# Experts kernel: four PSUM buffers for the second layer, the last addition of a tile on GpSimd, one Newton step fewer

## Chip, cores and metric

One core of a Trainium2 chip. The metric is the device time of one execution in microseconds; a version is judged by the median of its runs.

## What is computed

Two layers follow each other on x of 4 x 1024 x 256 (float32). The part that matters is the end of the second layer: a state-space block gives s, a mixture of experts gives g, and the output is x + s * g. Cut to that:

```python
residual = x                                    # xn, 4096 rows of 256
gate_weights = softmax(x @ gate_W + gate_b)     # 8 experts
topk_vals, topk_idx = top_k(gate_weights, 2)
boost = x
for i in range(2):                              # rank 0, rank 1
    h = relu(boost @ W1[e] + b1[e])             # e = topk_idx[..., i], 256 -> 512
    outs[i] = h @ W2[e] + b2[e]                 # 512 -> 256
    boost = boost + 0.5 * outs[i]
fused = topk_vals[0] * outs[0] + topk_vals[1] * outs[1]
g = silu(layer_norm(residual + fused, ln_gamma, ln_beta))
x = x + s * g
```

## The kernel before

The kernel first computes layer 0 (about 0 to 930 us of the profile), then the state-space scan (to about 1930 us), then the experts in two ranks. Only the experts are touched by the change.

Each rank sorts the 4096 rows by their expert and pads them to 39 tiles (NTILE) of 128 rows, every tile of one expert. Every engine has its own program, an order written out by hand, and waits for the others on semaphores.

A tile of a rank goes through these stages. GpSimd gathers its rows by an indirect DMA (first rank L1243, second rank L1276, `second_rows`) into one of six row buffers (NR). TensorE turns the tile (L1881, `turned_in`), ScalarE copies it out of PSUM (L1543) and picks the expert's first weights (L1552). TensorE makes the hidden layer (L1900, `hidden`), ScalarE applies bias and relu (L1561), and TensorE makes the second layer (L1913, `rows_out`) into a PSUM buffer pM2, of which there are two; before it overwrites one it waits on m2c until VectorE has read it. TensorE's order within a tile n is hidden(n + 1), turned_in(n + 2), rows_out(n).

In the first rank VectorE then runs `boost` (L1707, L1709, L1710), and SyncE stores the rows. In the second rank it runs `fuse` (L1726 adds the weighted bias, L1729 adds the product from PSUM, L1731 and L1732 make the statistics) into one of nine buffers f (NF); fuse(n) first waits until the output of tile n - 9 has landed. After every third tile it runs `normalise` on that group of three (GROUP): an inverse square root by a seed (L1736 to L1738) and four Newton steps (L1740 to L1742) on 128 x 3 numbers, then two passes over the three tiles (L1745, L1750). ScalarE applies silu (L1567). `finish` multiplies by s (L1756) and adds x (L1758); both come from `mx`, a ring of eight buffers (NX) that GpSimd fills by an indirect gather (L1281, `last_rows`). VectorE runs finish(n - 6) behind fuse(n), three times behind the last fuse, and three times more at the end. GpSimd scatters the finished tile to the output (L1285, `finished`).

GpSimd's queue in the second rank is a loop: in turn n it gathers the rows of tile n (waiting for turned_in and for fuse of tile n - 6), gathers mx for tile n - 4 (waiting for finish of tile n - 12), and scatters tile n - 12 (waiting for its finish). Turns 12 to 38 have all three, turns 39 to 42 the last two, turns 43 to 50 the scatter alone:

```python
for n in range(NTILE + 2 * LAG):                # LAG = 6
    if n < NTILE:
        second_rows(n)
    if 0 <= n - LAG + 2 < NTILE:
        last_rows(n - LAG + 2)
    if n >= 2 * LAG:
        finished(n - 2 * LAG)
```

The wait of L1284 stands, in the program that is built, on the instruction that loads the register for the scatter's bounds check, ahead of the DMA instruction; the wait of `last_rows` stands on its DMA instruction.

Of the kernel before, what the change touches and what calls it, by code (L numbers as in the profile page):

```python
# [9 lines left out]
ALU = mybir.AluOpType  # L10
# [3 lines left out]
B, L, D = 4, 1024, 256  # L14
P = 128
# [919 lines left out]
NTILE = 39  # L935
# [4 lines left out]
NR, NF, LAG, NX = 6, 9, 6, 8  # L940
# [5 lines left out]
def phase_me(nc, g):  # L946

    AT = half_jobs()
    with ExitStack() as ctx:
# [3 lines left out]
        def sem(name):  # L953
            return ctx.enter_context(nc.semaphore(name))
# [6 lines left out]
        def part(of, at, shape, dt=F32):  # L961

            n = int(np.prod(shape))
            v = of[:, at:at + n]
            v = v if dt is F32 else v.bitcast(dt)
            if len(shape) == 2:
                return v.rearrange("p (a b) -> p a b", b=shape[1])
            if len(shape) == 3:
                return v.rearrange("p (a b c) -> p a b c", b=shape[1], c=shape[2])
            return v  # L970
# [48 lines left out]
        e_w2 = [xi[:, :, :].rearrange("p m t -> p (m t)")[:, 0:E * D]] + [zu[:, k, :, :].rearrange("p a t -> p (a t)") for k in (1, 2, 3)]  # L1019
        b2 = zu[:, 4, :, :].rearrange("p a t -> p (a t)")  # L1020
        f = part(rows, 0, [NF, D])
        mx = part(rows, NF * D, [NX, 2 * D])
# [11 lines left out]
        row = lambda n: first[:, n % NR, :] if n % NR < 2 else rest[:, n % NR - 2, :]  # L1034
        xsT = tile([2, KD * P]); ws = tile([2, KD * HE]); hT = tile([2, HE])
        st = sb("st_e", [P, 2, GROUP, 6]); mv = sb("mv_e", [P, 2, GROUP, 2]); rs = sb("rs_e", [P, 4, GROUP]); spare = sb("spare_e", [P, 1])

        Q = [ctx.enter_context(nc.psum_tensor(f"m_Q{i}", [P, 2, CH], F32)) for i in range(4)]
        pT1, _, pM2, pT2 = Q
        dA, du, _, Y = (q[:, :, :].rearrange("p a b -> p (a b)") for q in Q)  # L1040
        X = [Q[2][:, i, :] for i in range(2)]
        R0, R1 = Q[3][:, 0, :], Q[3][:, 1, :]
# [15 lines left out]
        t1 = sem("e_t1"); t1c = sem("e_t1c"); picked = sem("e_picked")  # L1058
        t2 = sem("e_t2"); t2c = sem("e_t2c"); m2 = sem("e_m2"); m2c = sem("e_m2c")
        row_ok = sem("e_row_ok"); r1_out = [sem(f"e_r1_out{i}") for i in range(3)]  # L1060
        ln = sem("e_ln"); fn = sem("e_fn"); sl = sem("e_silu"); fin = sem("e_fin"); og_out = [sem(f"e_og_out{i}") for i in range(NF)]; f_out = sem("e_out")

        def tile_at(b, kind, m):
            return b * NQT + (TILES if b else TILES0).index((kind, m))
# [4 lines left out]
        with nc.Block() as block:  # L1069
# [78 lines left out]
            def _(pool):  # L1148
# [90 lines left out]
                def index(r, n, i):  # L1239
                    return bass.IndirectOffsetOnAxis(ap=ext[:, r, n, i:i + 1], axis=0)  # L1240
# [31 lines left out]
                def second_rows(n):  # L1272
                    if n >= NR:
                        pool.wait_ge(t1, NTILE + n - NR + 1)
                        pool.wait_ge(m2c, NTILE + n - NR + 1)
                    nc.gpsimd.indirect_dma_start(row(n), None, g["r1_s"], index(1, n, 0)).then_inc(r_in[n % NR], 16)  # L1276

                def last_rows(n):
                    if n >= NX:
                        pool.wait_ge(fin, 2 * (n - NX) + 2)  # L1280
                    nc.gpsimd.indirect_dma_start(mx[:, n % NX, :], None, g["mx_s"], index(1, n, 1)).then_inc(mx_in[n % NX], 16)  # L1281

                def finished(n):
                    pool.wait_ge(fin, 2 * n + 2)  # L1284
                    nc.gpsimd.indirect_dma_start(g["out"].rearrange("b n d -> (b n) d"), index(1, n, 2), f[:, n % NF, :], None, bounds_check=B * L - 1, oob_is_err=False).then_inc(og_out[n % NF], 16)  # L1285

                for n in range(NTILE + 2 * LAG):
                    if n < NTILE:
                        second_rows(n)
                    if 0 <= n - LAG + 2 < NTILE:  # L1290
                        last_rows(n - LAG + 2)
                    if n >= 2 * LAG:
                        finished(n - 2 * LAG)

            @block.scalar
            def _(ac):
# [288 lines left out]
            def _(dv):  # L1585
                v_ = nc.vector
# [13 lines left out]
                k = [2]  # L1600
# [97 lines left out]
                def boost(n):  # L1698
                    dv.wait_ge(m2, n + 1)
                    if n >= 3:  # L1700
                        dv.wait_ge(r1_out[n % 3], 16 * (n // 3))
                    w = ext[:, 0, n, 3:4].bitcast(F32)
                    if n == 0:
                        dv.wait_ge(b2_in, 16)
                    e = dv.value_load(texp[0:1, 0, n:n + 1], min_val=0, max_val=E - 1)
                    m = out1[:, n % 3, D:]
                    v_.tensor_tensor(m, pM2[:, n % 2, 0:D], b2[:, bass.ds(e * D, D)], ALU.add).then_inc(m2c, 1)  # L1707
                    dv.wait_ge(m2c, n + 1)
                    v_.scalar_tensor_tensor(out1[:, n % 3, 0:D], m, 0.5, row(n)[:, 0:D], ALU.mult, ALU.add).then_inc(row_ok, 1)  # L1709
                    v_.scalar_tensor_tensor(m, m, w, row(n)[:, 0:D], ALU.mult, ALU.add).then_inc(row_ok, 1)  # L1710
# [9 lines left out]
                def fuse(n):  # L1720
                    if n >= NF:
                        dv.wait_ge(og_out[n % NF], 16 * (n // NF))
                    w = ext[:, 1, n, 3:4].bitcast(F32)
                    e = dv.value_load(texp[0:1, 1, n:n + 1], min_val=0, max_val=E - 1)  # L1724
                    dv.wait_ge(r_in[n % NR], 16 * (turns_of[n % NR] + n // NR + 1))
                    link(v_.scalar_tensor_tensor(row(n)[:, D:], b2[:, bass.ds(e * D, D)], w, row(n)[:, D:], ALU.mult, ALU.add))  # L1726
                    dv.wait_ge(m2, NTILE + n + 1)
                    dst = f[:, n % NF, :]
                    v_.scalar_tensor_tensor(dst, pM2[:, (NTILE + n) % 2, 0:D], w, row(n)[:, D:], ALU.mult, ALU.add).then_inc(m2c, 1)  # L1729
                    dv.wait_ge(m2c, NTILE + n + 1)  # L1730
                    link(v_.bn_stats(st[:, n // 3 % 2, n % 3, :], dst))  # L1731
                    link(v_.bn_aggr(mv[:, n // 3 % 2, n % 3, :], st[:, n // 3 % 2, n % 3, :]))  # L1732

                def normalise(q):
                    var, y, y2 = (rs[:, i, :] for i in range(3))
                    link(v_.tensor_scalar(var, mv[:, q % 2, :, 1], EPS, None, ALU.add))  # L1736
                    link(v_.tensor_scalar(y2.bitcast(I32), var.bitcast(I32), 1, None, ALU.logical_shift_right))
                    link(v_.tensor_scalar(y.bitcast(I32), y2.bitcast(I32), -1.0, RSQRT_SEED, ALU.mult, ALU.add))  # L1738
                    for _ in range(4):
                        link(v_.tensor_tensor(y2, y, y, ALU.mult))  # L1740
                        link(v_.scalar_tensor_tensor(y2, y2, -0.5, var, ALU.mult, ALU.mult))  # L1741
                        link(v_.scalar_tensor_tensor(y, y2, 1.5, y, ALU.add, ALU.mult))  # L1742
                    for i in range(GROUP):
                        dst = f[:, (q * GROUP + i) % NF, :]
                        v_.scalar_tensor_tensor(dst, dst, mv[:, q % 2, i, 0:1], gamma[:, 0, :], ALU.subtract, ALU.mult).then_inc(ln, 1)  # L1745
                    c[0] += GROUP
                    dv.wait_ge(ln, c[0])
                    for i in range(GROUP):
                        dst = f[:, (q * GROUP + i) % NF, :]
                        v_.scalar_tensor_tensor(dst, dst, y[:, i:i + 1], gamma[:, 1, :], ALU.mult, ALU.add).then_inc(fn, 1)  # L1750

                def finish(n):
                    dv.wait_ge(sl, n + 1)
                    dv.wait_ge(mx_in[n % NX], 16 * (n // NX) + 16)
                    dst = f[:, n % NF, :]
                    v_.tensor_tensor(dst, dst, mx[:, n % NX, 0:D], ALU.mult).then_inc(fin, 1)  # L1756
                    dv.wait_ge(fin, 2 * n + 1)
                    v_.tensor_tensor(dst, dst, mx[:, n % NX, D:], ALU.add).then_inc(fin, 1)  # L1758

                for n in range(NTILE):  # L1760
                    boost(n)
# [11 lines left out]
            def _(pe):  # L1773
                mm = nc.tensor.matmul
# [87 lines left out]
                for b in range(B):  # L1862
                    for i in range(STEPS):
                        n = b * STEPS + i
                        m, s = divmod(i, NS)
# [38 lines left out]
                def rows_out(r, n):  # L1904
                    q = r * NTILE + n
                    e = pe.value_load(texp[0:1, r, n:n + 1], min_val=0, max_val=E - 1)
                    if q == 0:
                        pe.wait_ge(w2_in, 16 * HE // P)
                    pe.wait_ge(t2c, q + 1)
                    if q >= 2:  # L1910
                        pe.wait_ge(m2c, q - 1)
                    for k in range(HE // P):
                        ins = mm(pM2[:, q % 2, 0:D], hT[:, q % 2, k * P:(k + 1) * P], e_w2[k][:, bass.ds(e * D, D)],  # L1913
                                 start=(k == 0), stop=(k == HE // P - 1))
                    ins.then_inc(m2, 1)

# [77 lines left out]
```

## Time and profile before

| | us |
|---|---|
| median of 3 runs | 2315.36 (2309.3 to 2317.42) |
| the profiled execution | 2311.29 |
| its span, first to last instruction | 2309.6 |
| busy in the span: TensorE | 1934.5 |
| VectorE | 1716.8 |
| ScalarE | 1258.1 |
| GpSimd | 1225.2 |
| mean granted TensorE clock | 0.949 |

The median is what a change is compared with; durations of single instructions come from the profiled execution. Busy shares over the whole span say little about one stage, so the stages of the two ranks are looked at by themselves. PE is TensorE's matmuls, PEld its weight loads, DVE is VectorE, ACT ScalarE, POOL GpSimd, SP SyncE; a number in brackets is the time the engine sat idle before the instruction, and what ended it.

### The profile page before, as it was taken

The page shows a single profiled execution, that of the slowest core. Times are in us where ns is not written, and L with a number is a line of the kernel's source. Part 1 is how long each engine was busy: PE and PEld are TensorE (multiplying, and loading weights), DVE is VectorE, ACT ScalarE, POOL GpSimd, SP SyncE. Part 2 cuts the span into 40 slices and gives each one's busy share as a digit, 9 for nine tenths or more (in the row PEclk, how much of TensorE's full clock was granted, in tenths as well). Part 3 has the DMA queues.
Part 4 walks back from the last instruction along what each step waited for, and adds up shares of the span by engine and source line. Part 5 has one row for each costly group of instructions (what it writes and reads, how often), then busy time and mean ns, then how long its engine had stood idle before and what let it go on. Part 6 is the DMA issues. An engine that isn't in the chain of part 4 may idle for free. (4 is left out here: it accounts for less than half of the span.)

```text
span 2309.6 us, 25591 instructions
## 1 busy us (share of the span) xinstructions
PE 1934.5 (84%) x7956; PEld 1054.0 (46%) x7956; DVE 1716.8 (74%) x2363; ACT 1258.1 (54%) x1646; POOL 1225.2 (53%) x651
## 2 busy tenths in 40 slices
PE   5699879977997899889988998899876678998984
PEld 3335534643464345333324333433332235887873
DVE  4984498369826952699999999999989995333887
ACT  3873486258526741566654666466644334664663
POOL 2601351054106210278879899989986774223664
PEclk9899989999998999999998999999999999999997
DMA  6510641073007311688888988998899993223442
GB/s 163 138 37 0 156 108 29 0 198 76 19 19 182 74 37 47 69 313 282 287 287 295 308 289 262 317 318 283 266 289 377 331 327 132 98 97 106 138 136 79
DMA packets 182695, 402.63 MB, mean 174 GB/s; under 512 B 49454, under 2 KB 78384, under 8 KB 181410
## 3 DMA queue, kind: packets, MB, share of 16 engines
q1 hardware_dynamic: 170530, 371.10, 52.2%
q0 software_dynamic: 12032, 29.90, 4.5%
q8 instruction: 66, 1.08, 0.2%
q14 instruction: 67, 0.55, 0.1%
HBM read 356.30 MB, written 45.51 MB: 174 GB/s over the span
## 5 line engine op out<-in xcount | busy, mean ns | idle before, releaser
L1191 POOL TENSOR_TENSOR late<-late,rows 128x1024 f32<-128x1024 f32 x256 | 603.2, 2365 | 146.7 <-DVE late L1668 135.3
L1841 PE MATMUL m_Q<-late,ident_m 128*128 128x512 f32 x1024 | 526.6, 646 | 153.1 <-POOL late L1191 113.8
L1668 DVE TENSOR_TENSOR_SCAN late<-m_Q,late 128x1024 f32<-128x1024 f32 x256 | 586.3, 2290 | 45.1 <-ACT m_Q L1377 16.6
L1377 ACT ACTIVATE m_Q<-late,acol 128x1024 f32<-128x1024 f32 x256 | 286.1, 1118 | 362.8 <-DVE late L1668 360.6
L1841 PEld LDWEIGHTS m_Q<-late,ident_m 128*128 128x128 f32 x1024 | 194.3, 202 | 452.5 <-POOL late L1191 260.5
L1661 DVE TENSOR_TENSOR late<-m_Q,rows 128x1024 f32<-128x1024 f32 x256 | 307.2, 1200 | 12.8 <-DMA rows<-bc_s 12.6
L290 POOL TENSOR_TENSOR qkh<-early,qkh 128x1024 bf16<-128x1024 f32 x16 | 33.9, 2130 | 287.4 <-ACT qkh L561 287.4
L456 DVE SCALAR_TENSOR_TENSOR early<-early,work 128x1024 f32<-128x1024 f32 x128 | 155.9, 1218 | 25.2 <-ACT early L598 22.7
L1900 PE MATMUL m_Q<-late 128*128 128x128 f32 x1248 | 159.0, 282 | 8.0 <-DVE m_so L1696 0.8
L1900 PEld LDWEIGHTS m_Q<-late 128*128 128x128 f32 x1248 | 148.5, 194 | 32.7 <-issue 31.0
L606 ACT ACTIVATE early<-early 128x1024 f32<-128x1024 f32 x128 | 134.8, 1053 | 47.4 <-DVE early L461 46.1
L607 ACT ACTIVATE early<-early,halfpi 128x1024 f32<-128x1024 f32 x128 | 145.2, 1134 | 0.0
L493 DVE TENSOR_TENSOR s<-work,s 128x1024 f32<-128x1024 f32 x8 | 9.8, 1224 | 172.9 <-PE work L678 172.9
L461 DVE TENSOR_SCALAR early<-early 128x1024 int32<-128x1024 int32 x128 | 125.3, 979 | 4.4
L678 PE MATMUL work<-w,qkh 128*128 128x256 f32 x512 | 112.6, 381 | 10.8 <-ACT qkh L623 10.8
L332 POOL TENSOR_TENSOR rows<-kr 128x1024 f32<-128x1024 f32 x8 | 16.8, 2119 | 194.6 <-DVE kr L449 194.6
L1913 PE MATMUL m_Q<-m_zu,late 128*128 x468 | 115.0, 382 | 0.0
L840 PE MATMUL work<-x2T,w 128*128 128x512 f32 x256 | 111.6, 594 | 1.0 <-ACT x2T L538 1.0
L678 PEld LDWEIGHTS work<-w,qkh 128*128 128x128 f32 x512 | 96.6, 190 | 30.3 <-ACT qkh L623 17.5
L623 ACT ACTIVATE qkh<-work,b1c 128x512 f32<-128x512 f32 x64 | 40.5, 684 | 123.2 <-PE work L840 123.2
L1788 PE MATMUL m_Q<-early 128*128 128x512 f32 x224 | 106.4, 598 | 0.0
L1707 DVE TENSOR_TENSOR late<-m_Q,m_zu 128x256 f32<-128x256 f32 x39 | 16.6, 425 | 111.5 <-PE m_Q L1913 97.4
(231 smaller groups left out, 3375.1 us busy)
## 6 DMA issues: line engine op xcount, KB each, us to landing
rows<-bc_s SPq DMA_DIRECT2D x512, 512.0 KB, 5.7
rows<-st_s SPq DMA_DIRECT2D x64, 384.0 KB, 5.7
st_s<-qkh SPq DMA_DIRECT2D x128, 96.0 KB, 2.4
r_s<-late SPq DMA_DIRECT2D x39, 256.0 KB, 2.0
rows<-st_s SPq DMA_DIRECT2D x32, 256.0 KB, 6.5
xin<-in_x SPq DMA_DIRECT2D x4, 1024.0 KB, 10.2
xres<-in_x SPq DMA_DIRECT2D x4, 1024.0 KB, 7.2
mx_s<-s SPq DMA_DIRECT2D x4, 1024.0 KB, 4.5
```

Source lines behind the costliest of these rows:

```text
L456: v_.scalar_tensor_tensor(fs[:, s % NF_, :], fs[:, s % NF_, :], ROUND, slot(b, *job)[:, :], ALU.subtract, ALU.subtract).then_inc(rr_ok, 1)
L461: v_.tensor_scalar(fc[:, s % NF_, :].bitcast(I32), fs[:, s % NF_, :].bitcast(I32), 0x7FFFFFFF, None, ALU.bitwise_and).then_inc(ra_ok, 1)
L606: A(fs[:, s % NF_, :], fs[:, s % NF_, :], ACT.Sin, scale=-TURN).then_inc(feat_ok, 1)
L607: A(fc[:, s % NF_, :], fc[:, s % NF_, :], ACT.Sin, scale=-TURN, bias=halfpi[:, :]).then_inc(feat_ok, 1)
L678: i = mm(slot(b, *job)[:, t * D:(t + 1) * D], x(k, t), w[:, k, :], start=(k == 0), stop=(k == nk - 1))
L1191: nc.gpsimd.tensor_tensor(pr[:, n % NH, :], h[:, n % NH, :], cb[:, n % NCB, :], ALU.mult).then_inc(pr_ok, 1)
L1377: A(dA[:, :], dt[:, (b * KI + m) % 2, :], ACT.Exp, scale=acol[:, m, i % NS:i % NS + 1]).then_inc(dA_ok, 1)
L1661: v_.tensor_tensor(dB[:, n % 2, :], du[:, :], bb[:, n % NBB, :], ALU.mult).then_inc(dB_ok, 1)
L1668: v_.tensor_tensor_scan(h[:, n % NH, :], dA[:, :], dB[:, n % 2, :], 0.0, ALU.mult, ALU.add).then_inc(h_ok, 1)
L1841: ins = mm(half(Y, c), ident[:, :], half(pr[:, n % NH, :], c), start=False, stop=(n % NS == NS - 1), skip_group_check=True)
L1900: ins = mm(pT2[:, q % 2, m * P:(m + 1) * P], ws[:, q % 2, k * HE + m * P:k * HE + (m + 1) * P], xsT[:, q % 2, k * P:(k + 1) * P], start=(k ...
L1913: ins = mm(pM2[:, q % 2, 0:D], hT[:, q % 2, k * P:(k + 1) * P], e_w2[k][:, bass.ds(e * D, D)], start=(k == 0), stop=(k == HE // P - 1))
```

## The change

It has four parts. The product of the second layer goes to one of four PSUM buffers instead of two, in both ranks, and rows_out(q) waits for the reading of q - 4 instead of q - 2. The second one uses banks that before held a value of the scan. The addition of x in `finish` (L1758) goes from VectorE to GpSimd's `finished`, which now waits for the multiplication, adds, waits for its own addition on a new semaphore (last), and scatters; fin counts one per tile. In GpSimd's turn `finished` goes ahead of `last_rows`, which waits on last. The Newton loop has three steps instead of four.

```diff
-        pT1, _, pM2, pT2 = Q
+        pT1, pM2a, pM2b, pT2 = Q
+        product = lambda q: (pM2a, pM2b)[q // 2 % 2][:, q % 2, 0:D]
...
                 def last_rows(n):
                     if n >= NX:
-                        pool.wait_ge(fin, 2 * (n - NX) + 2)
+                        pool.wait_ge(last, n - NX + 1)
                     nc.gpsimd.indirect_dma_start(mx[:, n % NX, :], None, g["mx_s"], index(1, n, 1)).then_inc(mx_in[n % NX], 16)
 
                 def finished(n):
-                    pool.wait_ge(fin, 2 * n + 2)
+                    pool.wait_ge(fin, n + 1)
+                    nc.gpsimd.tensor_tensor(f[:, n % NF, :], f[:, n % NF, :], mx[:, n % NX, D:], ALU.add).then_inc(last, 1)
+                    pool.wait_ge(last, n + 1)
                     nc.gpsimd.indirect_dma_start(g["out"]...).then_inc(og_out[n % NF], 16)
 
                 for n in range(NTILE + 2 * LAG):
                     if n < NTILE:
                         second_rows(n)
+                    if n >= 2 * LAG:
+                        finished(n - 2 * LAG)
                     if 0 <= n - LAG + 2 < NTILE:
                         last_rows(n - LAG + 2)
-                    if n >= 2 * LAG:
-                        finished(n - 2 * LAG)
...
-                    v_.tensor_tensor(m, pM2[:, n % 2, 0:D], b2[:, bass.ds(e * D, D)], ALU.add).then_inc(m2c, 1)
+                    v_.tensor_tensor(m, product(n), b2[:, bass.ds(e * D, D)], ALU.add).then_inc(m2c, 1)
...
-                    v_.scalar_tensor_tensor(dst, pM2[:, (NTILE + n) % 2, 0:D], w, row(n)[:, D:], ALU.mult, ALU.add).then_inc(m2c, 1)
+                    v_.scalar_tensor_tensor(dst, product(NTILE + n), w, row(n)[:, D:], ALU.mult, ALU.add).then_inc(m2c, 1)
...
-                    for _ in range(4):
+                    for _ in range(3):
...
                     v_.tensor_tensor(dst, dst, mx[:, n % NX, 0:D], ALU.mult).then_inc(fin, 1)
-                    dv.wait_ge(fin, 2 * n + 1)
-                    v_.tensor_tensor(dst, dst, mx[:, n % NX, D:], ALU.add).then_inc(fin, 1)
...
-                    if q >= 2:
-                        pe.wait_ge(m2c, q - 1)
+                    if q >= 4:
+                        pe.wait_ge(m2c, q - 3)
                     for k in range(HE // P):
-                        ins = mm(pM2[:, q % 2, 0:D], hT[:, q % 2, k * P:(k + 1) * P], e_w2[k][:, bass.ds(e * D, D)],
+                        ins = mm(product(q), hT[:, q % 2, k * P:(k + 1) * P], e_w2[k][:, bass.ds(e * D, D)],
```

## Rows read from the trace of the kernel before

**Rows 1.** Busy time (instructions) of each engine in a stretch; PEclk, DMA share, GB/s.

```profile
1943.00:2085.61 142.61, 138.71 (x911) 120.26 (x910) 43.61 (x105) 86.00 (x208) 31.26 (x33) 1.00 0.28 96
2170.34:2268.46 98.12, 83.54 (x546) 73.17 (x546) 85.51 (x273) 58.73 (x148) 63.51 (x63) 1.00 0.46 139
```

**Rows 2.** Chain of waits, first rank: start us, us, what.

```profile
1946.83 2.02 PE m_Q L1900 x16
...
2081.54 2.02 PE m_Q L1900 x16
```

**Rows 3.** Timeline, VectorE in one group of the second rank: start, duration.

```profile
2199.47 0.43 DVE L1756 TENSOR_TENSOR rows<-rows 128x256 f32<-128x256 f32 x1
...
2199.93 0.42 DVE L1758 TENSOR_TENSOR rows<-rows 128x256 f32<-128x256 f32 x1
...
2206.80 0.17 DVE L1740 TENSOR_TENSOR rs_e<-rs_e 128x3 f32<-128x3 f32 x1
...
2207.40 0.16 DVE L1740 TENSOR_TENSOR rs_e<-rs_e 128x3 f32<-128x3 f32 x1
```

**Rows 4.** Timeline, GpSimd: its turn 12 begins, and one unhindered turn.

```profile
2143.35 0.95 POOL L1276 DMA_INDIRECT late<-r_s,ext  x1 [5.12 <-DVE rows L1729]
...
2161.75 0.98 POOL L1276 DMA_INDIRECT late<-r_s,ext  x1 [0.30 <-PE m_Q L1881]
2163.03 0.95 POOL L1281 DMA_INDIRECT rows<-mx_s,ext  x1 [0.30 <-DVE rows L1729]
2164.29 1.02 POOL L1285 DMA_INDIRECT out<-rows,ext  x1 [0.30 <-issue]
```

**Rows 5.** DMA issues from 2170 to 2268 us: count, median us from issue to landing.

```profile
late<-r_s,ext POOLq DMA_INDIRECT x21, 3.7
...
out<-rows,ext POOLq DMA_INDIRECT x21, 2.9
```

**Rows 6.** Groups by line and shape, GpSimd: count, busy us, mean ns of one.

```profile
L293 POOL TENSOR_TENSOR v<-v,bias 128x1024 f32<-128x1024 f32 x8 | 18.8, 2350 | 1.5 <-ACT v L567 1.5
L293 POOL TENSOR_TENSOR xn_a<-xn_a,bias 128x2048 f32<-128x2048 f32 x4 | 18.8, 4690 | 0.3
...
L317 POOL TENSOR_TENSOR rows<-rows 128x1024 f32<-128x1024 f32 x8 | 21.0, 2647 | 0.0
```

**Rows 7.** Timeline, GpSimd: distances between neighbours, in the scan and before it.

```profile
930.25 0.73 POOL L1162 IOTA ent<- 128x32 int32 x5
931.04 0.23 POOL L1164 MEMSET late<- 128x8 f32 x1
...
1603.09 1.00 POOL L1236 DMA_INDIRECT ext_s<-ent,pos  x1 [0.17 <-issue]
1604.12 4.68 POOL L1191 TENSOR_TENSOR late<-late,rows 128x1024 f32<-128x1024 f32 x2
1608.97 1.00 POOL L1236 DMA_INDIRECT ext_s<-ent,pos  x1 [0.17 <-issue]
```

**Rows 8.** Timeline, the last stretch: VectorE's results and the DMAs they release.

```profile
2276.02 0.43 DVE L1758 TENSOR_TENSOR rows<-rows 128x256 f32<-128x256 f32 x1
...
2276.71 0.98 POOL L1281 DMA_INDIRECT rows<-mx_s,ext  x1 [0.65 <-DVE rows L1758]
...
2298.78 0.43 DVE L1758 TENSOR_TENSOR rows<-rows 128x256 f32<-128x256 f32 x1
...
2300.00 1.19 POOL L1285 DMA_INDIRECT out<-rows,ext  x1 [4.43 <-DVE rows L1758]
...
2302.78 0.99 POOL L1285 DMA_INDIRECT out<-rows,ext  x1 [0.30 <-issue]
```

**Rows 9.** VectorE's L461: one beside GpSimd's L317 (timeline), and its group's mean.

```profile
741.50 1.60 DVE L461 TENSOR_SCALAR early<-early 128x1024 int32<-128x1024 int32 x1
...
L461 DVE TENSOR_SCALAR early<-early 128x1024 int32<-128x1024 int32 x128 | 125.3, 979 | 4.4
```

More of the change, by code:

```diff
@@ L1060, in phase_me @@
         row_ok = sem("e_row_ok"); r1_out = [sem(f"e_r1_out{i}") for i in range(3)]
-        ln = sem("e_ln"); fn = sem("e_fn"); sl = sem("e_silu"); fin = sem("e_fin"); og_out = [sem(f"e_og_out{i}") for i in range(NF)]; f_out = sem("e_out")
+        ln = sem("e_ln"); fn = sem("e_fn"); sl = sem("e_silu"); fin = sem("e_fin"); last = sem("e_last"); og_out = [sem(f"e_og_out{i}") for i in range(NF)]; f_out = sem("e_out")
         def tile_at(b, kind, m):
```

## The prediction

> **What bounds the kernel now.** I read the stage windows first, then the chain of waits, then the timelines of single engines. The change touches only the two expert ranks, about the last 370 us. In the first rank TensorE is busy for 138.71 of 142.61 us while VectorE works 43.61; in the second VectorE is busy 85.51 of 98.12 us and TensorE only 83.54 [rows 1]. The chain of waits says the same of the first rank: it is TensorE's, and a tile takes (2081.54 - 1946.83) / 33 = 4.08 us [rows 2]. The second window of rows 1 spans the fusions of tiles 12 to 33, 21 tiles or seven groups of three: 14.02 us per group, 4.67 per tile. The gaps between dependent instructions fill the rest of VectorE's time, so it never really rests. TensorE needs 3 x 4.08 = 12.24 per group and waits for the rest, some 1.8, on the PSUM buffer that fuse has to read first (m2c).
>
> GpSimd is the third engine to look at, since the change gives it work. Its turn is a gather, a gather of last rows and a scatter, 0.98 + 0.95 + 1.02 us with 0.30 ahead of each: 3.85 us when nothing holds it [rows 4]. In a group it needs 11.6 of the 14.02 us.
>
> **Part 1, VectorE's work taken away.** L1758 starts 0.46 us behind L1756 [rows 3]; without it all that follows moves up by that: 1.38 per group. One Newton step is the distance between two starts of L1740, 0.60 us [rows 3]. VectorE then needs 14.02 - 1.98 = 12.04 us per group, 4.01 per tile, just under TensorE's 4.08.
>
> **Part 2, four PSUM buffers.** The wait of rows_out moves from two to four tiles back, so the stall of 1.8 goes. With VectorE under TensorE's pace, two buffers would nearly do as well: I put nothing extra on it. In the first rank the wait never binds, for VectorE rests there; cost and gain 0. If only parts 1 and 2 counted, the 35 tiles behind the first group would take 4.08 instead of 4.67, and the end would come some 20 us earlier.
>
> **Part 3, GpSimd's addition.** Its turn becomes gather, addition, wait on its own semaphore (last), scatter, gather of last rows. Four prices:
> - The addition, 128x256. The same line costs 2350 ns for 1024 elements and 4690 for 2048 [rows 6], in proportion with nothing fixed, so 256 would be 0.59 to 0.60 us. Beside a busy VectorE the additions of L317 took 2647 for 1024 [rows 6], 1.13 times. As L1726, L1745, L1750 and L1756 will lie beside it, I take 0.66; lower end 0.59.
> - The start behind a gather: 0.03 (1603.09 + 1.00 to 1604.12) [rows 7].
> - From the addition to the scatter. Nothing in this trace waits on GpSimd itself before an indirect DMA, so it is bounded. A DMA that has nothing to wait for starts 0.17 behind an addition (1604.12 + 4.68 to 1608.97) [rows 7]. The gather of last rows, which waits directly, starts 0.27 after VectorE's result (2276.02 + 0.43 to 2276.71), but the scatter L1285, where the wait stands ahead of an instruction that loads its bounds, started at 2300.00 after a result at 2298.78 + 0.43 = 2299.21: 0.79 [rows 8]. The new wait stands in that very place, so the price is near 0.79. A tenth of it is VectorE's signal (0.27 against 0.17 without a wait), while a GpSimd instruction that waits for GpSimd starts some 0.06 behind it (930.25 + 0.73 to 931.04) [rows 7]; I take that tenth off, about 0.70. Ends: 0.17 and 0.82. Nothing can hide this gap: the queue is in order.
> - What it replaces: the 0.30 ahead of the scatter.
>
> A turn is then 0.98 + 0.03 + 0.66 + 0.70 + 1.02 + 0.30 + 0.95 + 0.30 = 4.94 us, over TensorE's 4.08 and over today's 4.65. GpSimd becomes the bound, and the moved order (finished ahead of last_rows) changes nothing in this sum: the gather of last rows waits for the same tile as before, and is needed only two tiles later.
>
> The Trainium skill (SBUF - State Buffer, section "Who interferes with whom") says that a VectorE instruction with two SBUF inputs and a GpSimd instruction that reads SBUF exclude each other, whoever is first. By that rule each of the four VectorE instructions named above could hold the addition off until it ends, and the addition could hold them off for 0.6; it speaks against this change. Of those four the trace shows none beside an addition; its nearest is L461, which took 1.60 us beside GpSimd's L317 against a mean of 0.979 over the kernel [rows 9].
>
> **The sum.** GpSimd is not bound before its turn 12, the first with a scatter; that turn began at 2143.35, when fuse(6) had run [rows 4]. Two norms lie ahead of fuse(6); the first gives back at most 0.4, since fuse(5) waits for its product anyway, the second 0.6: turn 12 starts at 2142.35. From there the queue holds 27 gathers at 1.28, 31 gathers of last rows at 1.25 and 39 scatters at 1.32, less the last 0.30: 124.5 us. Today they are spread until 2302.78 + 0.99 = 2303.77 [rows 8], because VectorE is the bound. The change adds to each of 39 scatters 0.03 + 0.66 + 0.70 - 0.30 = 1.09, 42.5 in all: 2142.35 + 124.5 + 42.5 = 2309.35, **5.6 us later** than 2303.77. What follows the last scatter is the same.
>
> Does anything else hold the queue? The gather of tile n waits for fuse(n - 6). fuse(n) waits for the scatter of n - 9, issued 2.37 us into turn n + 3 and landed 2.9 later [rows 5]; with some 1.8 for value load, L1726 and L1729 it is done about 7.1 into that turn, and turn n + 6 begins at 14.8. The 5 us of a norm fit between. The other way round, a gather needs 3.7 to land [rows 5], and its tile is fused some two turns of TensorE and one product later, about 18 us, 23 with a norm, against six turns of 29.6. At the end turn 38 begins at 2142.35 + 26 x 4.94 = 2270.8, so fuse(38) comes at about 2283 to 2288, and VectorE's last product some 8 us later, before GpSimd's turn for it at about 2302. So GpSimd runs without a pause, and TensorE and VectorE rest in every tile.
>
> The profiled execution took 2311.29 us around a span of 2309.6; the median of the runs is 2315.36, 4.1 above it. I add the difference to the median: 2315.36 + 5.6 = **2321.0 us**. A measurement of this kernel can tell about 0.3% (7 us) from no change, so this is the same time, on the slow side.
>
> **Rivals.**
> - **The addition meets VectorE's instructions (slower).** Place: the addition in each of 39 turns. If half of them wait out an instruction of 0.48, it costs 0.59 + 0.24 = 0.83 or a little more, 0.84: 39 x 0.18 = 7.0 on top, 2328.0. It decides from a mean of 0.695, where the sum passes 7 us. For it: L461 [rows 9]; against: 1.13 is all that L317 shows. [...]
> - **The own wait is cheap (faster).** If the scatter starts 0.30 behind the addition, like every DMA behind another, the turn is 4.54, under 4.65, and 39 x 0.40 = 15.6 us go: 10.0 under the kernel before, 2305.4. With 0.17 it is 2300.3. Against it: 0.79 at the same line.
> - **GpSimd keeps up and TensorE is the bound.** Then some 20 us are gained, 2295. It needs a turn of 4.08, but the three DMAs with the bare addition already are 3.86 + 0.60 = 4.46 less the 0.30 replaced, plus at least 0.20, which is 4.36. Hardly possible.
> - **TensorE loses its clock.** Resting 0.86 us of each 4.94 it could fall to the lower level; at full clock a tile is 4.08, at half about 8. The window of the second rank shows a granted clock of 1.00 with rests of 15% of its time [rows 1]; the rests here are 17%. A few tens of us if it came.
>
> **Chances.** Forecast 0.40; port contention 0.30; cheap wait 0.23; TensorE-bound 0.03; clock 0.04. The forecast's own bounds (addition 0.59 to 0.69, gap 0.66 to 0.76) are 2316.7 to 2324.5, nearly all within 0.3%. Range: 2303.5 to 2329 takes in the cheap wait and the contention. Faster by over 0.3%: 0.26. Within: 0.37. Slower: 0.37.
>
> **What would show it.** After: GpSimd's turn near 4.94 with no wait for another engine from turn 12 on, the scatter 0.70 behind the addition, the addition at 0.66; TensorE waiting for gathered rows rather than for L1729; no time of VectorE's in waits for GpSimd but for landed scatters; the chain of the second rank on GpSimd. Wrong if the gap is 0.3, if additions pass 0.70, or if the chain is still VectorE's.

## The result, and the profile after

The change makes the kernel slower: the median after is 2336.3 us against 2313.3 of the kernel before, run beside it, a ratio of 1.0096 [1.008, 1.0112], 23.0 us. The forecast was 5.6 us slower with an upper end of 2329. The direction was right; the size was four times the forecast and outside the range.

The profiled execution after took 2330.37 us around a span of 2328.2. Line numbers have moved: the scatter is L1288 (was L1285), GpSimd's addition L1286, its gathers L1277 and L1282, the multiplication of `finish` L1759 (L1756), `fuse` L1729 and L1732 (L1726, L1729), the passes of the norm L1748 and L1753 (L1745, L1750), the second layer L1914.

First the busy times over the whole span (busy us, share, instructions), from the page of the kernel after:

```profile
PE 1944.7 (84%) x7940; PEld 1061.8 (46%) x7956; DVE 1710.3 (73%) x2285; ACT 1258.3 (54%) x1646; POOL 1258.2 (54%) x690
```

GpSimd gained 33 us of work and VectorE lost only 6.5, although it was relieved of 39 additions of 0.426 and of a Newton step. The stage windows say more (columns as in [rows 1]):

```profile
1943.00:2082.50 139.50, 135.64 (x888) 117.29 (x886) 42.32 (x102) 85.05 (x206) 31.20 (x33) 1.00 0.29 98
2170.34:2278.00 107.66, 88.51 (x515) 75.00 (x513) 77.72 (x223) 55.05 (x139) 78.50 (x79) 0.94 0.40 119
```

In the first rank TensorE is busy for 97% of the window, as before [rows 1], so the buffers changed nothing that shows there. In the second, VectorE went from 85.51 busy in 98.12 us (87%) to 77.72 in 107.66 (72%); TensorE is busy for 82%. Neither is the bound. GpSimd's busy share is 73% only, and yet it is the bound, as its timeline shows (start, duration, what; in brackets the idle time before it and what ended it):

```profile
2174.90 0.95 POOL L1277 DMA_INDIRECT late<-r_s,ext  x1 [0.30 <-issue]
2175.87 0.73 POOL L1286 TENSOR_TENSOR rows<-rows 128x256 f32<-128x256 f32 x1
2177.44 1.01 POOL L1288 DMA_INDIRECT out<-rows,ext  x1 [0.83 <-POOL rows L1286]
2178.76 0.96 POOL L1282 DMA_INDIRECT rows<-mx_s,ext  x1 [0.30 <-issue]
2180.02 0.95 POOL L1277 DMA_INDIRECT late<-r_s,ext  x1 [0.30 <-issue]
2181.00 0.97 POOL L1286 TENSOR_TENSOR rows<-rows 128x256 f32<-128x256 f32 x1
2182.80 1.01 POOL L1288 DMA_INDIRECT out<-rows,ext  x1 [0.83 <-POOL rows L1286]
```

One turn, from gather to gather, is 5.12 us here (forecast 4.94); the next one, where the addition takes 0.97, is 5.37. All idle time in it is its own: 0.30 between two DMAs, 0.83 between the addition and the scatter. From turn 12 to the last scatter GpSimd waited for another engine for under 1 us of 184. The ends of that stretch:

```profile
2138.41 0.94 POOL L1277 DMA_INDIRECT late<-r_s,ext  x1 [4.53 <-DVE rows L1732]
...
2321.33 0.99 POOL L1288 DMA_INDIRECT out<-rows,ext  x1 [0.80 <-POOL rows L1286]
```

That is 2322.32 - 2138.41 = 183.9 us, against 2303.77 - 2143.35 = 160.4 before [rows 4, 8]: 23.5 more. Turn 12 began 4.94 us earlier than before, but 3.06 of that lies ahead of everything the change touches (the first gather of the second rank started at 2097.45 instead of 2100.51 in this execution); the rest, 1.9, is put down to the change. By that the change costs 23.5 - 1.9 = 21.6 us in these two executions, and 23.0 between the medians.

GpSimd's groups, from the lines of the two ranks (instructions, busy us, mean ns of one, idle us before them and what ended it):

```profile
L1288 POOL DMA_INDIRECT out<-rows,ext x39 | 42.0, 1076 | 32.3 <-POOL rows L1286 32.3
...
L1286 POOL TENSOR_TENSOR rows<-rows 128x256 f32<-128x256 f32 x39 | 34.0, 872 | 1.2 <-DVE rows L1759 0.4
```

The forecast gave the addition 0.66, the gap 0.70, the scatter 1.02. They are 0.872, 32.3 / 39 = 0.83, and 1.076. And VectorE's (in [rows 3] L1759 was L1756 with 0.43):

```profile
L1729 DVE SCALAR_TENSOR_TENSOR late<-m_zu,ext,late 128x256 f32<-128x256 f32 x39 | 22.5, 578 | 40.8 <-DMA out<-rows,ext 29.0 <-DMA late<-r_s,ext 6.3 <-DVE mv_e L1735 3.2
L1748 DVE SCALAR_TENSOR_TENSOR rows<-rows,mv_e,gamma 128x256 f32<-128x256 f32 x39 | 21.0, 592 | 0.5
L1753 DVE SCALAR_TENSOR_TENSOR rows<-rows,rs_e,gamma 128x256 f32<-128x256 f32 x39 | 20.0, 566 | 0.5
L1732 DVE SCALAR_TENSOR_TENSOR rows<-m_Q,ext,late 128x256 f32<-128x256 f32 x39 | 18.9, 484 | 13.9 <-PE m_Q L1914 12.7
L1759 DVE TENSOR_TENSOR rows<-rows 128x256 f32<-128x256 f32 x39 | 18.0, 473 | 1.4 <-ACT rows L1570 0.3
```

The first three were 483, 481 and 481 ns in the kernel before, L1759 was 427, L1732 was 484. So four of the large lines have grown by 46 to 111 ns, 13 us together, and one has not. That one reads PSUM and a single tensor in SBUF; the four read two in SBUF. The growth lies where an addition of GpSimd's lies beside the instruction: L1729 takes 0.54 to 1.27 us in the 15 tiles where one does, and 0.47 to 0.49 in the other 24; L1732 takes 0.48 either way. One such meeting, VectorE's two instructions and the addition:

```profile
2202.70 0.72 DVE L1729 SCALAR_TENSOR_TENSOR late<-m_zu,ext,late 128x256 f32<-128x256 f32 x1 [3.11 <-DMA out<-rows,ext]
2203.03 0.97 POOL L1286 TENSOR_TENSOR rows<-rows 128x256 f32<-128x256 f32 x1
2203.46 0.48 DVE L1732 SCALAR_TENSOR_TENSOR rows<-m_Q,ext,late 128x256 f32<-128x256 f32 x1
```

The waits from 2110 to 2320 (waiting line, what it waited for: us, times, longest):

```profile
POOL out L1288 <- POOL rows L1286: 31.5, 38, 0.9
DVE late L1729 <- DMA out<-rows,ext: 29.0, 14, 3.1
PE m_Q L1882 <- DMA late<-r_s,ext: 13.1, 15, 1.6
```

`fuse` waits for the scatter of tile n - 9 to land, and TensorE waits for gathered rows: both waits are on transfers that GpSimd issues late. The chain of waits of the second rank shows how this looks from the end (start, us, what; its longest pieces):

```profile
2230.89 0.98 POOL rows L1286
2232.70 2.57 DMA out<-rows,ext
2240.50 1.83 DVE rows L1748 x3
...
2247.40 0.99 POOL rows L1286
2249.21 2.57 DMA out<-rows,ext
2257.24 1.76 DVE rows L1748 x3
```

It goes from a scatter's landing to VectorE's norm and back to GpSimd, once in 16.5 us, three of GpSimd's turns. Read alone, it would suggest that VectorE shares the blame. But it comes back from VectorE to GpSimd at the gather L1282, which has 0.30 us of idle time ahead of it there, the same as a DMA that waits for nothing; from turn 12 on VectorE held GpSimd's queue up by 0.4 us in all, and itself rested 29.0 us for landings.

### The profile page after: what moved, and what is told of

It reads as the page before. It is cut to its first block and busy times, and to the rows that moved or that the text cites. A ratio compares the mean times of both kernels' runs of the same rounds, so it can differ in the third digit from the quotient of the medians.

```text
span 2328.2 us, 25534 instructions
## 1 busy us (share of the span) xinstructions
PE 1944.7 (84%) x7940; PEld 1061.8 (46%) x7956; DVE 1710.3 (73%) x2285; ACT 1258.3 (54%) x1646; POOL 1258.2 (54%) x690
## 5 line engine op out<-in xcount | busy, mean ns | idle before, releaser
L1671 DVE TENSOR_TENSOR_SCAN late<-m_Q,late 128x1024 f32<-128x1024 f32 x256 | 586.2, 2290 | 45.1 <-ACT m_Q L1380 16.5
L461 DVE TENSOR_SCALAR early<-early 128x1024 int32<-128x1024 int32 x128 | 124.2, 970 | 4.4
L678 PE MATMUL work<-w,qkh 128*128 128x256 f32 x512 | 112.6, 381 | 10.9 <-ACT qkh L623 10.9
L1914 PE MATMUL m_Q<-m_zu,late 128*128 x468 | 120.3, 396 | 0.0
L1914 PEld LDWEIGHTS m_Q<-m_zu,late 128*128 128x128 f32 x468 | 93.0, 199 | 13.8
```

The source lines that it names most:

```text
L461: v_.tensor_scalar(fc[:, s % NF_, :].bitcast(I32), fs[:, s % NF_, :].bitcast(I32), 0x7FFFFFFF, None, ALU.bitwise_and).then_inc(ra_ok, 1)
L678: i = mm(slot(b, *job)[:, t * D:(t + 1) * D], x(k, t), w[:, k, :], start=(k == 0), stop=(k == nk - 1))
L1671: v_.tensor_tensor_scan(h[:, n % NH, :], dA[:, :], dB[:, n % 2, :], 0.0, ALU.mult, ALU.add).then_inc(h_ok, 1)
L1914: ins = mm(product(q), hT[:, q % 2, k * P:(k + 1) * P], e_w2[k][:, bass.ds(e * D, D)], start=(k == 0), stop=(k == HE // P - 1))
```

## The experiments

Each ratio is to the kernel before on the same chip, with its 95% interval in brackets. On the chip of a to d, e2, m2, n2 and t that kernel took 2311 to 2312 us; p and the first runs of e, m and n were on another.

**a. The addition back on VectorE** (and the old order; four buffers and three Newton steps stay). It separates GpSimd's part from the rest.

```diff
-                    nc.gpsimd.tensor_tensor(f[:, n % NF, :], f[:, n % NF, :], mx[:, n % NX, D:], ALU.add).then_inc(last, 1)
-                    pool.wait_ge(last, n + 1)
...
+                    dv.wait_ge(fin, 2 * n + 1)
+                    v_.tensor_tensor(dst, dst, mx[:, n % NX, D:], ALU.add).then_inc(fin, 1)
```

> Four buffers and three Newton steps kept, the addition back on VectorE and GpSimd's order as before. Theory Q (GpSimd's own in-order turn of 5.3 us is what made the changed kernel slow): the turn falls back to 3.85 and VectorE is the bound with 14.02 - 0.60 = 13.4 us per group; 12 groups x 0.6 = 7 us under the kernel before, about 2306. Rival P (the four buffers or their banks cost something by themselves): 2313 or more.

Measured: 2300.9, 0.9955 [0.994, 0.9969], 10.9 us under the median of the kernel before, and 5 under what was expected. The addition on GpSimd thus costs some 35 us against leaving it where it was, and parts 1 and 2 are a gain. Most groups of three took 13.3 to 13.4 us, against 14.02 less one Newton step of 0.60, 13.42.

**b. No addition at all** (the output lacks x).

```diff
-                    nc.gpsimd.tensor_tensor(f[:, n % NF, :], f[:, n % NF, :], mx[:, n % NX, D:], ALU.add).then_inc(last, 1)
-                    pool.wait_ge(last, n + 1)
```

> The changed kernel with the last addition left out altogether (the output lacks x), so that neither VectorE nor GpSimd pays for it. Theory Q: no engine but TensorE is near its limit, 4.08 us per tile, about 20 us under the kernel before, 2293. Rival L (it is the landing of the scatters, for which fuse waited 29 us in the changed kernel, and the ring of nine buffers that bound it, whatever the addition): VectorE goes on waiting for landings and the time stays near 2313 or above.

Measured: 2287.6, 0.9894 [0.9878, 0.9911], 24 us faster. That is what the change would have been worth had GpSimd's part been free; the forecast had put it at about 20, and the expectation at 2293. Waits for landings (the rival) are not what bound the changed kernel.

**c. The bounds register loaded once.** In the built program the wait on `last` stands on the instruction that loads the register for the bounds check, and the load then stands between the wait and the DMA. Here the register is loaded ahead of the loop, and the wait stands on the DMA itself:

```diff
+                top = pool.to_reg(B * L - 1)
...
-                    nc.gpsimd.indirect_dma_start(... bounds_check=B * L - 1, oob_is_err=False)
+                    nc.gpsimd.indirect_dma_start(... bounds_check=top, oob_is_err=False)
```

> The changed kernel with the bound of the scatter's bounds check loaded into its register once, so that the wait on the own addition stands on the DMA instruction itself. Theory Q: the 0.83 us between addition and scatter fall to 0.2 to 0.3, the addition stays at 0.87; 39 x 0.55 = 21 us less than the changed kernel, about 2315. Rival S (it is the semaphore from GpSimd to itself that takes 0.8): no change, 2336.

Measured: 2316.2, 1.0016 [1.0003, 1.0029], 20 us less than the same kernel with the load in place (d, below). GpSimd's timeline, the addition's line now L1288, the scatter's L1290:

```profile
2174.77 0.99 POOL L1288 TENSOR_TENSOR rows<-rows 128x256 f32<-128x256 f32 x1
2176.03 1.01 POOL L1290 DMA_INDIRECT out<-rows,ext  x1 [0.28 <-POOL rows L1288]
```

The gap fell from 0.83 to 0.28. 39 x 0.55 = 21.5 us were to go, and 19.6 went: nearly each microsecond taken out of GpSimd's queue shows in the time, as it must if that queue is the bound. The edit changes two things at once, where the wait stands and whether a load follows it, and they were not tried apart.

**d. Two buffers again**, all else as changed.

```diff
-        product = lambda q: (pM2a, pM2b)[q // 2 % 2][:, q % 2, 0:D]
+        product = lambda q: pM2b[:, q % 2, 0:D]
...
-                    if q >= 4:
-                        pe.wait_ge(m2c, q - 3)
+                    if q >= 2:
+                        pe.wait_ge(m2c, q - 1)
```

> The changed kernel with two PSUM buffers again. Theory Q: TensorE rests in every tile anyway, so the time is that of the changed kernel, 2336, within 4. Rival P (the buffers decide something): TensorE's old stall of 1.8 us per group comes on top of GpSimd's turns, up to 12 x 1.8 = 21 us, 2357; or, if the banks cost, less than 2332.

Measured: 2335.8, 1.0107 [1.0088, 1.0125], the changed kernel's time as expected. The four buffers do nothing that can be told, good or bad, while GpSimd is the bound.

**e, m, n, p on another chip.** There the kernel before took 2346.6 (no trace of it was kept), and e, m and n show pauses of 3 to 9 us in which TensorE and ScalarE rested, which make their second ranks some 20 to 40 us longer than those of e2, m2 and n2. In p there is one such wait, of 3.6 us. From the waits of n:

```profile
ACT late L1544 <- remote: 50.2, 10, 8.9
```

The trace names no cause for them. A gain or loss of VectorE's can vanish in such pauses, so e, m and n were run again on the first chip, as e2, m2 and n2, with the kernels unchanged. Their first runs are told by their ratios only: e 0.9948 [0.9928, 0.9967], m 0.9979 [0.9965, 0.9992], n 0.9995 [0.9979, 1.0011]. Those of e and n do not agree with e2 and n2: on that chip e was faster than the kernel before, and n was not. What follows on these two holds for the first chip.

> The changed kernel's work, in another order in GpSimd's turn: the addition of tile n - 12 first, then the gather of rows, the gather of last rows, and the scatter last, so that two DMAs lie over the wait (in the last turns the next tile's addition lies over it). Theory Q: the gap of 0.83 is covered, the gather starts about 0.2 behind the addition, so the turn is about 4.65; 39 x 0.7 = 27 us less than the changed kernel, 2309. If the gap is not covered (rival S, GpSimd's sequencer doesn't run ahead of its own wait): 2336.

> As the one before, but only every second addition of the first 30 tiles on GpSimd, 15 of 39, the others on VectorE. Theory Q: VectorE needs 13.35 - 1.5 x 0.46 = 12.7 us per group and GpSimd 3 x 3.85 + 1.5 x 0.8 = 12.8, both near TensorE's 12.2: 4.25 per tile, under the 4.45 of the run with all additions on VectorE; about 6 us less than that one, 2295. Rival C (the exclusion at the port costs VectorE what it is spared: each addition holds it up by up to 0.5): no gain on 2301.

> The kernel before with three Newton steps instead of four, and nothing else. Theory Q: VectorE's group falls from 14.0 to 13.4 us, 7 us in all, the same as with four buffers, 2301 to 2306. Rival P (four buffers bring something of their own while VectorE is the bound): at least 3 us slower than the run a_add_on_vectore.

**p. A write in place of the addition.** `memset` writes zeros to the tile where GpSimd added (the output is zeros). It keeps the turn's shape, with its own wait, but reads nothing from SBUF.

```diff
-                    nc.gpsimd.tensor_tensor(f[:, n % NF, :], f[:, n % NF, :], mx[:, n % NX, D:], ALU.add).then_inc(last, 1)
+                    nc.gpsimd.memset(f[:, n % NF, :], 0.0).then_inc(last, 1)
```

> The changed kernel with the addition replaced by an instruction of GpSimd that reads nothing: it fills the tile with zeros (the output is not the sum). The wait and the scatter stay. Theory C (a GpSimd instruction that reads SBUF and a VectorE instruction with two SBUF inputs exclude each other; it made 0.73 into 0.87 and VectorE's L1729, L1748, L1753 longer): the fill takes its bare 0.46 in every tile and VectorE's three lines are back at 0.48. The turn is 5.34 - 0.41 = 4.93, 16 us less than the changed kernel, 2320. Rival (GpSimd's instructions get longer whatever they do, by the DMAs' traffic): both stay long.

Measured on the second chip: 2313.7, 0.9865 [0.9845, 0.9885]. The durations decide here, not the time. The groups from 2130 to 2330:

```profile
L1729 DVE SCALAR_TENSOR_TENSOR late<-m_zu,ext,late 128x256 f32<-128x256 f32 x33 | 15.9, 483 | 16.7 <-DMA out<-rows,ext 8.5 <-issue 8.1
L1748 DVE SCALAR_TENSOR_TENSOR rows<-rows,mv_e,gamma 128x256 f32<-128x256 f32 x36 | 15.5, 485 | 0.4
L1753 DVE SCALAR_TENSOR_TENSOR rows<-rows,rs_e,gamma 128x256 f32<-128x256 f32 x36 | 15.4, 481 | 0.4
```

They are back at the kernel before's lengths, 481 to 485 (595, 602 and 573 in the changed kernel over the same window). The write took 0.332, and the gap stayed:

```profile
2177.61 1.02 POOL L1288 DMA_INDIRECT out<-rows,ext  x1 [0.83 <-POOL rows L1286]
```

The fill does meet them: 11 of the L1729 lie beside one, and each takes 0.48. So these lines grow by GpSimd's reading of SBUF, and the gap is the same behind an instruction that reads nothing and takes 0.33. The fill itself is shorter than the 0.46 expected.

**e2. The own wait covered.** The addition goes to the front of the turn, so that two gathers lie between it and the scatter (order: addition n - 12, gather n, last rows, scatter n - 12).

```diff
+                def plus(n):
                     pool.wait_ge(fin, n + 1)
                     nc.gpsimd.tensor_tensor(...).then_inc(last, 1)
+
+                def finished(n):
                     pool.wait_ge(last, n + 1)
...
+                    k = n - 2 * LAG
+                    if 0 <= k <= NTILE - NX:
+                        plus(k)
                     if n < NTILE:
                         second_rows(n)
```

> The kernel of e_wait_covered again, on the chance of another chip: in the last four runs, the kernel before among them, the second rank was some 30 us longer than in the runs ahead of them, with up to ten pauses of 3 to 9 us in which ScalarE did nothing though its input was there, so that what they say of GpSimd's turn and VectorE's group is overlaid. Without such pauses, theory Q: GpSimd's turn is 4.5 to 4.6 (addition 0.77, gather 0.16 behind it), VectorE's group 12.1 plus the port's share, so about 4.6 per tile at most: 2300 to 2309, a ratio of 0.995 to 0.999.

Measured: 2312.5, 1.0007 [0.9998, 1.0017], 23 us less than d, but a few us over the upper end of what was expected. From its timeline:

```profile
2196.35 0.76 POOL L1286 TENSOR_TENSOR rows<-rows 128x256 f32<-128x256 f32 x1
2197.27 0.99 POOL L1277 DMA_INDIRECT late<-r_s,ext  x1 [0.16 <-POOL rows L1286]
...
2200.83 0.90 POOL L1286 TENSOR_TENSOR rows<-rows 128x256 f32<-128x256 f32 x1
```

The gap is gone, and a turn is 4.48 here. VectorE's group now sets the pace at least as much as GpSimd's turn, for its instructions meet the additions (its groups; L1755 is the norm's first pass, L1736 the bias line):

```profile
L1736 DVE SCALAR_TENSOR_TENSOR late<-m_zu,ext,late 128x256 f32<-128x256 f32 x39 | 24.6, 632 | 17.6 <-issue 6.7 <-DMA late<-r_s,ext 6.2 <-DVE mv_e L1742 3.2
L1755 DVE SCALAR_TENSOR_TENSOR rows<-rows,mv_e,gamma 128x256 f32<-128x256 f32 x39 | 23.9, 666 | 0.5
```

They are 149 and 185 ns longer than before. VectorE's group is 13.6 us (between the starts of two norms' first passes), three of GpSimd's turns are 13.4: what was lifted off VectorE, 0.43 a tile, it pays back in longer instructions. From 2095 to 2330 us it is busy for 157.45 us, and in n2 (below), which has all 39 additions on it, for 153.61. The expectation had not charged that in full. This is read from the durations; how the missing microseconds divide between the two engines was not tried.

**m2 and t. A part of the additions on GpSimd**, covered as in e2: every second tile of the first 30 (m2, 15 additions), every third (t, 10); VectorE does the others.

```diff
+BY_POOL = range(0, 30, 2)                       # t: range(1, 30, 3)
...
+                def plus(n):
+                    if n in BY_POOL:
+                        pool.wait_ge(fin, n + 1)
+                        nc.gpsimd.tensor_tensor(...).then_inc(last, 1)
```

> The kernel of m_half_of_additions again. Theory Q, without the pauses: VectorE 12.7 us per group plus some 0.2 for the port, GpSimd 12.8: 4.3 per tile, 2293 to 2298, ratio 0.992 to 0.994, below all additions on VectorE (0.9955). Rival C (the port costs VectorE what it is spared): 0.9955 or more.

> As m2_half_of_additions, with one addition in each group of three on GpSimd (10 of 39). Theory Q: VectorE 13.35 - 0.46 + 0.1 = 13.0 us per group, GpSimd 12.4: 4.33 per tile, 2295 to 2300; between half and none.

Measured: m2 2304.8, 0.9979 [0.9968, 0.999]; t 2302.6, 0.9964 [0.9951, 0.9978]. Both expectations were missed (2293 to 2298 and 2295 to 2300), and the rival of m2, that the port costs VectorE what it is spared, came. In the middle of the rank m2's groups of three take 12.7 to 13.0 and 14.2 to 15.2 us by turns, where a's take 13.3 to 13.5. The medians rise with the additions on GpSimd (39: 2312.5, 15: 2304.8, 10: 2302.6, none: 2300.9); 10 is not to be told from none.

**n2. The Newton step alone**: the kernel before with one line changed.

```diff
-                    for _ in range(4):
+                    for _ in range(3):
```

> The kernel of n_newton_alone again. Theory Q, without the pauses: 0.6 us less in 12 of VectorE's groups, ratio 0.997, 2304 to 2306, and with four buffers (0.9955) the same within the intervals. Rival P: 0.999 or more, so that four buffers made a_add_on_vectore's gain.

Measured: 2301.6, 0.9959 [0.9945, 0.9972]. VectorE's norm:

```profile
2188.45 0.17 DVE L1741 TENSOR_TENSOR rs_e<-rs_e 128x3 f32<-128x3 f32 x1
2189.04 0.17 DVE L1741 TENSOR_TENSOR rs_e<-rs_e 128x3 f32<-128x3 f32 x1
2189.64 1.28 DVE L1746 SCALAR_TENSOR_TENSOR rows<-rows,mv_e,gamma 128x256 f32<-128x256 f32 x3
...
2203.31 1.28 DVE L1746 SCALAR_TENSOR_TENSOR rows<-rows,mv_e,gamma 128x256 f32<-128x256 f32 x3
```

A step is 0.59 to 0.60, the group shown 13.67, others 13.3 to 13.5; from the first norm to the last there are 163.1 us in n2 and 162.4 in a. The time is that of a, which has the four buffers as well: 2301.6 and 2300.9, with overlapping intervals, so the step carries the gain of both as far as can be told (within some 4 us). This one-line change beats the kernel before by 9.7 us and the changed one by some 34; no run that does the whole computation was faster by more than the intervals.

## Why the forecast was too low

**Right: the mechanism.** GpSimd's queue, which is in order, became the bound; its turn is longer than what VectorE and TensorE need for a tile. TensorE waits for gathered rows and `fuse` for landed scatters, as forecast; c shows it by experiment, since time taken from that queue alone comes off the total. The predicted sign "the chain of the second rank on GpSimd" holds only in part: the chain comes back to GpSimd in every group of three but leaves it through landings and VectorE. That GpSimd never rests was the better sign.

**Right: parts 1 and 2.** The Newton step is 0.60 a group (n2, a). Four buffers were put at nothing: d against the changed kernel, and n2 against a, show nothing beyond their intervals. Parts 1 and 2 without GpSimd's work were put at some 20 us, and b gave 24.

**Wrong: the prices of the addition and of the gap behind it, and a little that of the scatter.** They were put at 0.66 + 0.70 + 1.02 us and took 0.872 + 0.83 + 1.076 in the mean of 39 tiles. The queue's stretch was to take 124.5 + 42.5 = 167.0 us, and took 183.9, 16.9 more. By the groups above:

- The addition, 0.66 forecast, 0.872 measured: 39 x 0.21 = 8.3 us. The prediction's own sign, additions over 0.70, came. Two things lie in it. Even alone it is not 0.59: the four with no instruction of VectorE's beside them (from 2284.98 us on) take 0.75, and the shortest of all 0.722. Going in proportion from 1024 and 2048 elements [rows 6] down to 256 missed some 0.15. The three sizes lie on no one line, so what makes up that part is open. The rest, 0.12 in the mean, goes with VectorE's instructions: 22 of the 39 take 0.92 to 1.00, and the median is 0.952. The 0.66 had taken this share from L317, 1.13 times; and L461, the row shown for the exclusion, has one SBUF input and is not of the kind of the four.
- The gap ahead of the scatter, 0.70 forecast, 0.83 measured: 5.0 us. The row at that very place said 0.79 [rows 8]. Taking a tenth off it, because a GpSimd instruction hears GpSimd sooner than it hears VectorE [rows 7], had no ground: 0.83 lies even above the upper end of 0.82. Where a GpSimd instruction waited for GpSimd, 0.06 was read off an IOTA and a MEMSET, not off a DMA. With the wait on the DMA instruction the same difference is 0.28 (c) against 0.27 [rows 8], so there is nothing to take off there either.
- The scatter itself, 1.02 forecast, 1.076 measured: 2.2 us. It takes 1.01 in some turns and 1.13 in others; why was not tried.

These are 15.5 of the 16.9. Turn 12 began 1.9 us earlier for the change instead of 1.0, which gives 0.9 back.

**The rivals.** The port contention, at 0.30, was right in mechanism, and its 0.84 for the addition is near the measured 0.872, in part by luck, since it starts from 0.59 and adds 0.24, where 0.75 and 0.12 were found; with the gap of 0.70 it still gave only 2328. The rule of the Trainium skill's page SBUF - State Buffer (section "Who interferes with whom") is borne out by the large instructions: lines with two SBUF inputs grow, L1732 with one does not, and a GpSimd instruction that only writes leaves them alone (p). What the forecast took from it was one side, the hold on the addition; the hold on VectorE, 13 us of longer instructions, was free in the changed kernel, where VectorE rests, but it weighs in e2, which on the first chip is no faster than the kernel before. The cheap wait did not come: 0.30 would have needed the register load out of the way. In c it is out of the way, at 0.28, and c is still not faster than before: the addition takes 0.861 there, 0.20 more than that rival had assumed (7.8 of the 10.0 us that it would have gained), and GpSimd waited for VectorE three times after its turn 12, some 5 us in all. TensorE was not the bound. Its granted clock was 0.94 in the second rank's window instead of 1.00, as the rival on the clock had it, but GpSimd's queue waited for TensorE nowhere, so the clock could not set the end; in c, with less rest, the same window shows 1.00.

**What stays open**: why an addition of 256 elements takes 0.75 us alone; whether the load or the place of the wait makes the 0.83; the cause of the pauses on the second chip; and the few microseconds by which e2 missed.

## What to carry to other kernels

Before giving work to an engine that looks idle, write down one turn of its in-order queue with all gaps, in particular a wait on its own result right ahead of a DMA: here 0.83 us of silence per tile cost as much as the addition itself, at a busy share of 73%. Look where the wait stands in the built program: with the register loaded ahead of the loop the wait stood on the DMA, and 0.55 us per tile went for one line of code. An addition moved from VectorE to GpSimd comes back in part as longer VectorE instructions if those read two tensors from SBUF; test the one-line part of a mixed change alone, for here it held all of the gain that could be told.

## What the runs showed of the hardware

- An indirect DMA that follows its own engine's result by a semaphore starts 0.83 us later if the wait stands on a register load ahead of it (the load itself takes 0.03), 0.28 if the DMA takes the wait itself; 0.16 behind an addition that it needn't wait for.
- A small VectorE instruction with one SBUF input can be caught too. In the changed kernel, beside an addition of GpSimd's from 2288.87 to 2289.60:

```profile
2289.02 0.61 DVE L1740 TENSOR_SCALAR rs_e<-rs_e 128x3 int32<-128x3 int32 x1
2289.67 0.17 DVE L1741 TENSOR_SCALAR rs_e<-rs_e 128x3 int32<-128x3 int32 x1
```

  L1740 takes 0.17 in most groups, as the line behind it does here; this time it ended where the addition ended. L1741, a tensor_scalar too, takes 0.17 in every group, but it never lies beside an addition; in c the same line took 0.65 once, beside a scatter. The Trainium skill's page SBUF - State Buffer (same section) counts tensor_scalar among the operations that can take the shared ports; these rows agree.
- Not only additions hold such an instruction. In the kernel before, one ended where the scatter beside it ended, and in p three L1740 took 0.32 to 0.33 beside the fill:

```profile
2149.73 1.03 POOL L1285 DMA_INDIRECT out<-rows,ext  x1 [0.31 <-issue]
2150.30 0.45 DVE L1737 TENSOR_SCALAR rs_e<-rs_e 128x3 int32<-128x3 int32 x1
```

- A GpSimd addition of 128x256 takes 0.75 us with nothing of VectorE's beside it and up to 1.00 beside VectorE in the changed kernel, where 1024 elements took 2.35 [rows 6]; the fill of the same size takes 0.33 in p.
